# Two-layer adaLN feed-forward kernel: the second layer's weights prepared in pieces inside the routed stage, and the order behind that stage interleaved

## What is computed

```python
x = x + _L0_ffn_ref(_L0_cond_ref(x, itok_B_0_7, L0_cond_weights, ...), ...)
x = x + _L1_ffn_ref(_L1_cond_ref(x, L1_cond_W, L1_cond_A, L1_cond_Bm, L1_cond_scalings, itok_B_0_6),
                    L1_ffn_w_gating, L1_ffn_w_linear)
```

## Time and profile before

| | |
|---|---|
| time before, median of 3 runs | 483.3 us (482.01 to 484.27) |
| the profiled execution's own time | 485.15 us |
| its span | 483.0 us |
| PE busy | 446.0 us (92%) |
| DVE busy | 312.0 us (65%) |
| ACT busy | 232.8 us (48%) |
| POOL busy | 242.8 us (50%) |

### The profile page before, as it was taken

The page is one execution under the profiler, slowest core; times in us unless marked ns, Lnnn a source line. Parts: engine busy times, 40 slices in busy tenths (PEclk is TensorE's granted clock), DMA queues, the critical chain, the costliest instruction groups (busy, mean ns, idle before and its releaser), DMA issues.

```text
span 483.0 us, 8723 instructions
## 1 busy us (share of the span) xinstructions
PE 446.0 (92%) x2777; PEld 367.0 (76%) x2777; DVE 312.0 (65%) x678; ACT 232.8 (48%) x459; POOL 242.8 (50%) x234
## 2 busy tenths in 40 slices
PE   1898997898987899999999999997999999999996
PEld 0698885787766799999999999786575675566563
DVE  5687479668761655555555555486678678667745
ACT  1446142344321355555555555432548547647744
POOL 5541304299996644444444440287307557557110
PEclk9999598899997999999999999997999999999999
DMA  7998000000001345555555464223203324214101
GB/s 237 356 342 287 22 2 0 1 1 0 1 1 44 110 148 163 149 164 148 164 148 163 148 161 109 79 85 99 65 2 109 92 61 121 88 56 130 45 28 61
DMA packets 35211, 50.60 MB, mean 105 GB/s; under 512 B 4210, under 2 KB 30066, under 8 KB 34920
## 3 DMA queue, kind: packets, MB, share of 16 engines
q1 hardware_dynamic: 28072, 31.91, 19.4%
q0 software_dynamic: 6528, 17.83, 14.0%
q10 hardware_dynamic: 576, 0.37, 0.3%
HBM read 32.27 MB, written 17.83 MB: 104 GB/s over the span
## 4 chain that ended last, share of the span: by engine, by line
PE 70%; POOL 12%; DVE 11%; ACT 2%; DMA 2%; issue 2%; SPq 0%; DVEq 0%; POOLq 0%
PE bank L1186 12%; PE bank L944 12%; POOL places L341 11%; PE bank L945 11%; PE bank L946 11%; PE bank L1205 6%; PE bank L1075 3%; PE bank L1097 3%; PE bank L953 3%; PE bank L975 3%; PE bank L1113 2%; PE bank L1112 2%; DVE bd L583 2%; PE bank L1152 1%; DMA xres<-in_x 1%
## 5 line engine op out<-in xcount | busy, mean ns | idle before, releaser
L350 POOL DMA_INDIRECT xg<-kept,perm x72 | 69.3, 963 | 72.8 <-PE bank L1075 60.3
L341 POOL TENSOR_SCALAR places<-cst,placef 128x72 f16<-128x72 f32 x64 | 55.5, 886 | 14.9 <-DVE xsl L605 14.9
L1186 PE MATMUL bank<-h,wg 128*128 128x512 fp8e4 x256 | 61.6, 381 | 0.8 <-DVE h L867 0.8
L795 DVE TENSOR_TENSOR hrl<-bank,hrh 128x256 fp32r<-128x256 f32 x36 | 15.3, 425 | 61.5 <-ACT hrh L464 61.5
L944 PE MATMUL bank<-w13h,xgl 128*128 x144 | 49.5, 344 | 0.6 <-DVE xgl L780 0.6
L1186 PEld LDWEIGHTS bank<-h,wg 128*128 128x128 fp8e4 x256 | 22.2, 98 | 34.8 <-ACT ff L520 14.7
L360 POOL DMA_INDIRECT ga<-slots_out,slot x32 | 34.1, 1065 | 28.1 <-SPq L308 19.5
L946 PE MATMUL bank<-w13h,xgh 128*128 x144 | 46.4, 322 | 0.0
L945 PE MATMUL bank<-w13l,xgh 128*128 x144 | 46.2, 321 | 0.0
L944 PE MATMUL bank<-xsh,sw13l 128*118 128x512 f32 (+1 forms) x96 | 41.2, 429 | 2.9 <-DVE hsf L644 2.9
L518 ACT ACTIVATE gel<-bank 128x512 bf16<-128x512 f32 x64 | 40.5, 633 | 5.8 <-PE bank L1186 2.8
(11 more groups left out here) (176 smaller groups left out, 1208.1 us busy)
## 6 DMA issues: line engine op xcount, KB each, us to landing
slots_out<-yr SPq DMA_DIRECT2D x36, 256.0 KB, 2.1
xres<-in_x SPq DMA_DIRECT2D x8, 512.0 KB, 8.9
kept<-xtr SPq DMA_DIRECT2D x7, 512.0 KB, 6.8
out_x<-fin SPq DMA_DIRECT2D x7, 512.0 KB, 2.8
w13raw<-in_rw SPq DMA_DIRECT2D x1, 2816.0 KB, 19.9
w2raw<-in_rw SPq DMA_DIRECT2D x1, 2048.0 KB, 26.0
wgst<-in_wgate SPq DMA_DIRECT2D x16, 128.0 KB
xg<-kept,perm POOLq DMA_INDIRECT x72, 3.1
```

The costliest lines, as they stand in the source:

```text
L341: pool.tensor_scalar(places[:, c, :], cst[:, C_J:C_J + SLOT_TILES], placef[:, c:c + 1], cst[:, C_TOKEN + t:C_TOKEN + t + 1], ALU.is_equal, ...
L350: pool.indirect_dma_start(out=xg[:, i % 2, j, :], out_offset=None, in_=kept, in_offset=bass.IndirectOffsetOnAxis(perm[:, 2 * i + j:2 * i + ...
L1186: ins = pe.matmul(bank[bk][:, :], wg8[:, kk, half, c * P:(c + 1) * P], h8[:, k, kk, :], start=(kk == 0), stop=(kk == KC - 1))
```

## The change

The raw weights still come in 16 steps, but each step's 256 columns of `wg8` and 128 columns of `wl8` are cast by DVE inside the routed stage (`cast_step(p)` behind `routed_mul(2p+2)`), with a semaphore pair `st_in` for the loads and a semaphore `w_cast` for the casts. The step's loads stand one step earlier on SP (`load_step(p)` behind the store of pair 2p-1), so that step 0 stands directly behind the load of `l1st`. The copy `l1h` becomes four pieces of 256 columns on ACT (behind pairs 4 to 7), its low part `l1l` four pieces on DVE (behind pairs 5, 7, 9 and 11). For that the loops of ACT, DVE and SP are written out. Behind the routed stage DVE's order for group 0's combine and group 7's hidden values is interleaved, `add_shared` of group 7 moves behind `to_h8`, and on PE two chunks of group 7's `shared_down` stand behind `mid_T` and the third behind `adapters_up`.

```diff
+WG_COLS = KC * 2 * HID // W_STEPS
+WL_COLS = HC * D // W_STEPS
+L1_PARTS = 4
@@ SP
-            with sp.Fori(1, PAIRS // 2 - 1) as half:
...
+            def load_step(p):
+                if p >= 2:
+                    sp.wait_ge(s("w_cast"), p - 1)
+                for st, src, cols in ((wgst, wgate, WG_COLS), (wlst, wlin, WL_COLS)):
+                    sp.dma_start(st[:, p * cols:(p + 1) * cols], src[:, p * cols:(p + 1) * cols]).then_inc(st_in[p % 2], 16)
+            for i in range(PAIRS):
+                if i % 2 == 0 and i // 2 < W_STEPS:
+                    load_step(i // 2)
                 sp.wait_ge(s("y_kept"), i + 1)
                 sp.dma_start(slots_out_t[i], yr[:, i % 2]...).then_inc(y_out[i % 2], 16)
@@ ACT
+            def second_hi(q):
+                act.wait_ge(s("l1_in"), 16)
+                act.activation(l1h[:, q, :], l1st[:, q, :], ACT.Copy).then_inc(s("l1_hi"), 1)
+            for i in range(1, PAIRS - 1):
+                routed(i, (i + 1) % 2, i <= 2)
+                if 4 <= i < 4 + L1_PARTS:
+                    second_hi(i - 4)
...
             shared_x_hi(EARLY + 1)
-            act.activation(l1h[:, :, :]..., l1st[:, :, :]..., ACT.Copy).then_inc(s("l1_hi"), 1)
             shared_act(EARLY + 1, hidden_late)
@@ DVE
+            for i in range(1, PAIRS - 1):
+                routed_h_lo(i - 1)
+                routed_x_lo(i + 1, (i + 1) % 2)
+                routed_mul(i)
+                if i % 2 == 0 and 2 <= i < 2 + 2 * W_STEPS:
+                    cast_step((i - 2) // 2)
+                if i % 2 == 1 and 5 <= i < 5 + 2 * L1_PARTS:
+                    second_lo((i - 5) // 2)
...
             add_shared(EARLY)
-            dve.tensor_scalar(wg8..., wgst[:, :], FP8_MAX, -FP8_MAX, ALU.min, ALU.max, saturate=False)
-            dve.tensor_scalar(wl8..., wlst[:, :], FP8_MAX, -FP8_MAX, ALU.min, ALU.max, saturate=False)
-            dve.tensor_tensor(l1l..., l1st..., l1h..., ALU.subtract)
...
+            first_a(0)
+            hidden_mul(EARLY + 1, 0, hidden_late)
+            first_a(1)
+            hidden_lo(EARLY + 1, 0, hidden_late)
+            combine_b(0, 0, 0)
+            hidden_mul(EARLY + 1, 1, hidden_late)
+            first_a(2)
+            hidden_lo(EARLY + 1, 1, hidden_late)
+            combine_b(0, 0, 1)
+            first_a(3)
+            hidden_mul(EARLY + 1, 2, hidden_late)
+            combine_b(0, 0, 2)
+            combine_b(0, 0, 3)
+            hidden_lo(EARLY + 1, 2, hidden_late)
             x_lo(0)
-            add_shared(EARLY + 1)
             xa_mask(0)
             xa_lo(0)
             to_h8(0, 0)
+            add_shared(EARLY + 1)
@@ PE
             shared_up(EARLY + 1)
-            shared_down(EARLY + 1, hidden_late, chunks=[0])
             mid_T(0, 0, True)
-            shared_down(EARLY + 1, hidden_late, chunks=[1, 2])
-            pe.wait_ge(s("l1_ready"), 2)
+            shared_down(EARLY + 1, hidden_late, chunks=range(2))
+            pe.wait_ge(s("l1_ready"), L1_PARTS)
+            pe.wait_ge(s("w_cast"), W_STEPS)
             adapters_down(0)
             linear(0, 0)
             linear(0, 1)
             adapters_up(0)
+            shared_down(EARLY + 1, hidden_late, chunks=[2])
```

## The result

The changed kernel takes 478.02 us (median of 4 runs, 477.89 to 479.05), the kernel before, on the same chip, 483.78 (482.01 to 484.5). The ratio is 0.9883, 95% interval 0.9857 to 0.9908. The forecast was 477.7, range 475.8 to 480.3. The profiled execution took 479.05 us with a span of 477.2 (before: 485.15 and 483.0).

What follows compares the result with a forecast made beforehand. PE was taken to bound the kernel, except behind the routed stage, where DVE's casts and combine held it up. Terms -6.1 + 0.15 + 0.3 = -5.65 us from 483.3 gave about 477.7 us, range 475.8 to 480.3.

Steps and rivals of the forecast that it cites:

- The place behind the stage: Between routed stage and first feed-forward: the feed-forward would begin at 338.7 in place of 344.81, 6.1 us earlier.
- The clock: Behind the routed stage PE's granted clock would stay up across the new gap; 2.3 of the 6.1 us hang on it.
- rival (a): The clock falls in PE's new gap behind the routed stage: 2.3 us back, 480.0 us; chance 0.08.
- The first feed-forward: There the moved add_shared of group 7 makes ACT's third gel late: 0.15 us of loss, at most 0.5.
- `xg` of pair 2: At the routed stage's start, step 0's 192 KB of load delay this gather: 0.3 us, between 0 and 0.7.
- the middle: The 0.3 us taken for step 0's delay of pair 2's gather, between 0 and 0.7.
- The routed stage: DVE's added casts, 0.35 us a step, hide in its 1.70 us of idle time before hrl and cost nothing.
- ACT's pieces: Four copies of 256 columns between yr and hrh in the routed stage: 0 taken, at most 0.3 each, 1.2 us.
- The loads: In the routed stage a load has 5.8 us from issue to cast; landings of 2.1 to 5.0 fit.
- Rival (c): Loads land late in the routed stage, so DVE stands before casts: at 7.7 us to landing 485.9 us; chance 0.05.
- The sum: Whole kernel: -6.1 + 0.15 + 0.3 = -5.65 us, from 483.3 to about 477.7 us.

Runs made afterwards that it cites:

- Experiment 6: Against the kernel before: changed kernel again 0.988; weight pieces with old orders 0.9912; new orders with long casts 0.996; changed kernel with three more edits 0.9849.
- experiment 3: Changed kernel with only weight step 0's load waiting for pair 2's transposes, l1st as before: 477.99 us, ratio 0.9871 to the kernel before.
- order only: Kernel before with the new DVE and PE orders behind the routed stage, weights still cast in one piece: 488.86 us on the slower chip, later 482.08 (0.996).
- experiment 4: Changed kernel with each step's two casts made 4 and 7 times, copies into spare memory: 477.88 and 488.54 us, one run each.
- experiment 5: Changed kernel with each weight load step issued one pair later on SP: 480.54 us, one run.

## Why the prediction was right, point by point

**The place behind the stage.** The mechanism was right, the size 0.3 too small: 6.1 forecast, 6.41 measured. The last `xm` was laid out 9.1 us behind the end of `add_shared` of group 6 (319.28 to 328.36) and came 9.2 behind it (319.87 to 329.08). PE stood 0.81 us in one piece, where 1.3 were laid out in all, and its eight transposes ended 0.2 earlier behind `add_shared` than forecast (329.32 - 319.87 = 9.45 against 9.67). The third chunk of `shared_down` covers `to_h8` as forecast: the last `h` is ready at 338.50, the feed-forward begins at 338.98 without a wait.

**The clock.** Right: 1.00 in all stretches, so rival (a) did not come. Experiment 6 shows which part keeps the clock up, in one trace of each: the pieces do it alone, the order alone doesn't. "TensorE: Matmul & The Clock Gate", Part 1, in the Trainium skill, says that idle stretches let the slow clock in. The traces agree where PE stood for 0.75 and 2.34 us and for 1.94 and 1.00, and do not show it at 0.81, at 1.43 and 0.35, nor at 1.80 before pair 2.

**The first feed-forward.** 0.15 forecast, a wait of 0.23 (0.24 in the second trace). Its begin to the span's end is 0.03 longer, so even this is mostly given back.

**`xg` of pair 2.** The mechanism was right; the size, 0.3 taken between 0 and 0.7, was too small: the distance is 0.47 longer, and step 0's bytes cost about 0.5 (experiment 3). The gather's own issue took 0.96 us here in place of 2.00 (below), but that is worth little: order only, with the start of the kernel before and an issue of 0.95 and 0.96, has 6.53 and 6.49 against 6.58. My reason for the middle, that the bytes stand behind `l1st`'s and `xg` has another queue, did not hold. The Trainium skill, "DMA: Bandwidth & Descriptors", in the section on queues, rings and completion order, has each DMA engine take its queues in turn, packet by packet. By that rule the bytes of a load in one queue can cost a gather in another queue time as long as both have work. The traces agree: 5.11, about 6.5 and about 7.0 us with no load, with `l1st` and with step 0 besides.

**The routed stage.** Right: nothing leaked. A step costs 0.34 us of cover (0.35 forecast), and experiment 4 shows the cover as real: the time moves once 1.36 us are used up. ACT's pieces are free: `l1h`'s piece of 0.41 us (at 180.96) lies between `yr` and `hrh`, and `hrh` starts 0.88 behind `yr` (180.46, 181.34), as in the pair before without a piece (176.44, 177.32). The prediction's own numbers did not give that: 0.60 + 0.30 is 0.90, past the 0.79 after which `hrh` starts, and it took 0 all the same. The piece fits because it starts 0.50 behind `yr`, whose row reads 0.60. From the stage's pair 2 to `add_shared` of group 6 it is 0.09 us shorter than before.

**The loads.** Rival (c) did not come: landings of 2.5 to 4.1 us within 5.8. Its price has a slip (7.7 us to landing gives 0.55 x 16 = 8.8, less 5.65 is 3.15 slower, not 2.4), and it was argued with one landing time for all 16 steps; experiment 5 shows that the steps differ. There the window is 5.8 - 4.0 = 1.8 us, and with the cover a landing of 3.2 should be free; the usual one (2.7) was, the slow three (4.1 to 4.5 with the issue, in the chain) were not.

**The sum.** -5.65 us forecast, -5.80 by the spans and -5.76 by the medians (483.78 to 478.02). That it is so close is in part luck: the place gave 0.31 more than forecast and the first feed-forward and the rest of the stage lost 0.21 less, while `xg` cost 0.17 more and 0.20 came ahead of pair 0, which no term had. The start of pair 0's transposes lies anywhere between 153.95 and 157.32 in the traces, and the interval of the ratio leaves the gain between 4.5 and 6.9 us.

## What to carry to other kernels

Where another engine bounds a stage and this one has a regular gap in it, a long preparation can be cut into pieces that fit the gap. Measure the gap as the idle time before the instruction that ends it, and the pieces with their fixed part. As long as the pieces fit, the price is nothing; beyond that the whole excess is paid once a round. Size the slack of a load by the longest landing, not by the median. And look at what a load that is issued early runs beside: here two loads that nothing was waiting for ran beside one gather. Put behind it, they let pair 2 start 2.0 us earlier, and the stage got 1.3 us shorter, because the next result in line, `hr`, then came last.

## What the runs showed of the hardware that had not been expected

**POOL's issue beside DVE.** Issuing the gather of pair 2 took 2.00 us before, 0.96 after. DVE and POOL of the kernel before, then of the changed one:

```profile
157.75 1.22 DVE L605 TENSOR_TENSOR xsl<-xtT,xsh 128x1024 fp32r<-128x1024 f32 x1
...
157.79 2.00 POOL L350 DMA_INDIRECT xg<-kept,perm  x1 [3.04 <-PE bank L1075]
```

```profile
157.99 0.96 POOL L354 DMA_INDIRECT xg<-kept,perm  x1 [2.73 <-PE bank L1107]
...
158.04 1.22 DVE L610 TENSOR_TENSOR xsl<-xtT,xsh 128x1024 fp32r<-128x1024 f32 x1
```

DVE's subtraction began 0.04 us ahead of POOL in the one and 0.05 behind it in the other; where DVE was first, POOL's issue took 1.04 longer, nearly the rest of the subtraction. This is not the change's doing: in the other twelve traces, order only among them, whose start is that of the kernel before, POOL was first by 0.02 to 0.07 us and its issue took 0.94 to 0.97. The Trainium skill, "GPSIMD Engine Reference", section 8, says that POOL shares its interfaces to SBUF with VectorE and contends there with an instruction that has two inputs in SBUF, as this one has. The traces agree, and show that it hangs on which of the two begins first. The long casts, which have one input, do it too. One gather of the kernel before was issued as `wg`'s cast began:

```profile
319.20 2.44 POOL L360 DMA_INDIRECT ga<-slots_out,slot  x1 [0.30 <-issue]
```

Order only has 2.49 and 2.45 at the same place. Without the long cast there no gather's issue behind the stage takes over 1.4 us up to 330.

**The clock and short gaps.** PE stood for 1.80 us before pair 2, and for 1.43 and 0.35 with two transposes between, and the granted clock stayed at 1.00; behind 1.94 and 1.00, and behind 0.75 and 2.34, it fell to 0.50 and to 0.52. Each is one execution, and no run varied the gap alone, so these are cases, and no bound.

**One chip's stretch without a cause.** On the slower chip engines took up finished work up to 13.6 us late, for the most part while POOL issued gathers. That instructions came late is not borne out: in the worst case it is ACT that takes up PE's finished transposes at 344.27, and of the two queues that the page calls "instruction" one (q8, 25 transfers in all) shows a transfer at 322 to 324 and the next past 364, the other none in that time; in the changed kernel on the other chip it is likewise 322 to 324 and the next at 348. The Trainium skill, "Runtime: NRT & Kernel Launch", in its section on how instructions are fetched, says that they come in blocks, fetched while the engine executes, and calls the price of going from one block to the next mostly hidden; nothing here speaks against it. The cause stays open: a run with the gathers held back on that chip would tell, and was not made.
